# Moving Silu of z one group later and small vector work to ScalarE in a fused Mamba and mixture-of-experts kernel

## The chip, the core and the metric

The kernel runs on one core of a Trainium2 chip. The metric is device time in microseconds (us) for one launch, as a median of repeated runs. A profiled execution of the same program gives the trace; its own time stands beside its span in the table below.

## What is computed

Input `x` is 8 sequences of 1024 tokens with 256 features, float32. Two sublayers run, each with layer norm before and after:

```
x = x + layernorm(mamba(layernorm(x)))
x = x + layernorm(moe(layernorm(x)))

mamba(x): xz = rms_norm(x) @ in_proj;  xb, z = split(xz)          # 512 channels each
          xc = silu(causal_conv4(xb));  dt, B, C = xc @ x_proj
          dt = softplus(dt * w + b)
          h_t = exp(dt*A) * h_(t-1) + dt * B * xc                  # 16 states per channel
          y = (sum_s h*C + xc*D) * silu(z);  return y @ out_proj + x
moe(x):   scores = sigmoid(x @ gate.T); best 2 of 4 groups, best 4 of 16 experts
          comb = chosen scores / their sum
          return sum_e comb_e * down_e(silu(gate_e x) * (up_e x))
```

## The kernel before

**Stages and groups.** The 8192 tokens are cut into 16 chunks of 512 (two to a sequence). The program is one software pipeline written out by hand: every engine walks the same list of stages `p` (-2 to 17), each of 16 groups `g`, and at each group issues what a list of `if` lines gives it. In stage `p` the scan of chunk `p` runs. Beside it stand the norm and transposes of the input of chunk `p+2` (functions `e_...`), the projections, convolution and activations of chunk `p+1` (`f_...`), the output projection, second norm and routing of chunk `p-1` (`p_...`), one expert a group for the chunks before (`gate`, `up`, `down`, `tanh`, `expert_gate`, `expert_up`, `weigh`), and the last norm (`z_...`). Experts start in group 10 of stage 1. Scans run in stages 0 to 15.

**One group on each engine.** A group is four (channel, state) tiles of 128x512. VectorE (DVE) does `expert_gate` (L1146), scan 0 (L1051), `expert_up` (L1151), scans 1, 2 and 3, then what the group has of its own, then `inputs` of the next group (L1037), a multiply of 128x2048. ScalarE (ACT) makes the factors exp(dt*A) for the scans (`decay`, L592) into two PSUM tiles, `dA0` and `dA1`, so the factor of a scan can only be made when the scan two before it is done. In group g it issues factors 2 and 3 of g, then a first lot of other work, then factors 0 and 1 of g+1, then `tanh` of the expert (L598), then a second lot. GpSimd multiplies the states with C and weighs experts. TensorE (PE) does `add_states`, `gate`, `up`, a first lot, `down` of the expert two groups before, and a second lot. Every engine runs its own list strictly in this order.

**Even and odd stages.** In an odd stage scans start from a kept state (form `hs<-dA,carry,hs`), in an even one ScalarE keeps the last column after `tanh` (`keep_ends`, L687, tile carry).

**Places that the change touches.**
- Silu of z: `f_silu_z` (L662), in the second lot of group 12 on ScalarE. z is copied out of PSUM before by `f_z` (L654), its last quarter in the first lot of group 12. Silu and Exp lie in different activation tables, so an `ACT_TABLE_LOAD` stands on each side of it; Copy, Identity and Square need no load, Exp and Tanh share one table.
- Input transposes: `e_turn` q=0 and q=1 on TensorE (L398), both in group 13, into the one PSUM bank FP (both halves use it in turn); ScalarE copies each out by `e_xT` (L630), q=0 in the second lot of group 13, q=1 in the first lot of group 14. `f_in` for 'b0' in group 14 needs both.
- Squares: `e_squares` (sum of squared differences from the mean, for chunk p+2), in the second lot of group 3; `z_squares(p-3)` in the first lot of group 3; `p_squares` 0 and 1, in the second lot of group 3 and the first of group 4. All write their squares to the tile DX and the sums to n_sq (the line of the squares themselves is L602, or L713 for `p_squares`).
- Variances and roots: VectorE turns sums into variances (L984, L976) and runs eight small dependent steps of Newton's method (`newton`, L958 to L972): `norms` at the end of group 4, `p_scale2` at the end of group 6, `z_scale` in the last stages.
- Routing: `route_groups` and `route_experts` on VectorE at the end of group 9, 26 small instructions; the last (L1142) scales the chosen scores into `comb`. TensorE turns `comb` in group 10 (L475), ScalarE copies it out (L753).
- The gate of y: `y_out` (L1058) at the end of groups 1, 5, 9 and 13 on VectorE. `conv` (2.3 us, L1004) is at the end of groups 2 and 3, in stages -1 to 14.

Of the kernel before, what the change touches and what calls it, by code (L numbers as in the profile page):

```python
# [85 lines left out]
def sandwich_kernel(nc, x, w_in, w_out, w_gu, w_dn, w_x, w_rt, cols, alog, ebias, consts, sel_dt, out):  # L86
    with ExitStack() as ctx:
# [20 lines left out]
        def channels(t, c):  # L108
# [72 lines left out]
        n_dve = Steps(sem('n_dve'), ['var_r', 'var'] + rsqrt_names('r') + ['nb'])  # L181
        e_act = Steps(sem('e_act'), ['sum', 'nm', 'sq', 'xr'])
        f_act = Steps(sem('f_act'), ['xT0', 'xT1', 'raw0', 'tap0', 'raw1', 'tap1', 'raw2', 'tap2', 'raw3', 'tap3', 'z0', 'silu_x', 'xd', 'dt', 'z1', 'z2', 'z3', 'silu_z'],
            ['xT0', 'xT1', 'raw0', 'tap0', 'raw1', 'tap1', 'raw2', 'raw3', 'tap2', 'tap3', 'silu_x', 'z0', 'xd', 'dt', 'z1', 'z2', 'z3', 'silu_z'])
# [195 lines left out]
        def _(pe):  # L380
# [157 lines left out]
            for p, g, G in groups():  # L538
# [23 lines left out]
                if in_e(p) and g == 13:  # L562
                    e_turn(p, 0)
# [12 lines left out]
                if in_e(p) and g == 13:  # L576
                    e_turn(p, 1)
# [5 lines left out]
        def _(act):  # L583
# [20 lines left out]

            dx_half = [flat[:, (TB + b) * DM:(TB + b + 1) * DM] for b in range(TB)]
# [8 lines left out]
            def e_squares(c):  # L614
# [5 lines left out]
                squares(xin, n_sq[:, 0:TB], n_nm[:, c % 4, TB:2 * TB], dx_half).then_inc(e_act.sem, 1)  # L620

# [83 lines left out]
            def p_squares(p, k):  # L705
# [42 lines left out]

            def p_cmT(p):
# [3 lines left out]
                act.activation(cmT[:, :], FP[0:NE, :], ACT.Copy).then_inc(p_act.sem, 1)  # L753
# [10 lines left out]
            def z_squares(c):  # L764
                if c < NC - 2:
                    act.wait_ge(st_dx, 16 * min(c + 4, NC))
                    nm, sq, waste = (n_nm[:, (c + 5) % 4, 3 * TB:], n_sq[:, 2 * TB:], dx_half)
                else:
                    act.wait_ge(st_dt, 16 * NC)
                    act.wait_ge(f_dve.sem, f_dve.at(NC - 1, 'dx'))  # L770
                    nm, sq, waste = (z_s[:, 2, :], z_s[:, 1, :], xb_half)
# [3 lines left out]
                squares(my, sq, nm, waste).then_inc(z_act.sem, 1)  # L775

# [42 lines left out]
            for p, g, G in groups():  # L819
# [48 lines left out]
                if 0 <= p + 2 < NC and g == 3:  # L868
                    e_squares(p + 2)
# [68 lines left out]
        def _(dve):  # L938
# [36 lines left out]
            def variance(v, sq):  # L975
                return dve.tensor_scalar(v, sq, 1.0 / DM, LN_EPS, ALU.mult, ALU.add)  # L976

            def norms(p):
# [3 lines left out]
                if E:  # L982
                    dve.wait_ge(e_act.sem, e_act.at(i, 'sq'))
                    dve.tensor_scalar(n_v[:, 0:TB], n_sq[:, 0:TB], (1.0 + RMS_EPS) / DM, LN_EPS * RMS_EPS, ALU.mult, ALU.add).then_inc(n_dve.sem, 1)  # L984
                if Z:
                    dve.wait_ge(z_act.sem, z_act.at(p - 3, 'sq'))
                if R_:
                    dve.wait_ge(p_act.sem, p_act.at(p - 1, 'sq'))
                v0 = max(c0, TB)
                variance(n_v[:, v0:c1], n_sq[:, v0 - TB:c1 - TB]).then_inc(n_dve.sem, 1 if E else 2)  # L990
                dve.wait_ge(n_dve.sem, n_dve.at(i, 'var'))
# [23 lines left out]
            def f_dx(p):  # L1015
# [5 lines left out]
                if in_p(p):  # L1021
                    dve.wait_ge(p_dve.sem, p_dve.at(p - 1, 'comb'))
# [89 lines left out]
            def route_experts(p):  # L1112
# [136 lines left out]
```

## Time and profile before

| what | value |
|---|---|
| median of 3 runs | 2586.57 us (2585.44 to 2588.78) |
| the profiled execution: its time | 2586.42 us |
| its span in the trace | 2584.6 us |
| busy: PE, DVE, ACT, POOL | 2365.7, 2375.5, 1607.1, 1495.0 us |
| stage 7, from its `f_dx` group on (1179.9 to 1329.5) | 149.6 us |

Times in the trace are from the start of the span. "PE", "DVE", "ACT" and "POOL" are TensorE, VectorE, ScalarE and GpSimd. A timeline row gives start, duration, engine, line, operation, output and inputs, how many instructions are merged in it, and in brackets how long the engine sat idle before it and what released it. An instruction's duration reaches about 0.1 us into the next one of its engine, so costs are best taken from start to start.

### The profile page before, as it was taken

Reading aid. Unit: us, or ns where it says so; the run is one execution under the profiler, and the core shown is the slowest. Engines: PE = TensorE matmul, PEld = TensorE weight load, DVE = VectorE, ACT = ScalarE, POOL = GpSimd, SP = SyncE. Lnnn points to the kernel's source line nnn. Section 1 sums busy time; section 2 is a strip of 40 time slices with the busy share of each in tenths; the row PEclk is TensorE's granted clock in tenths of the full one; section 3 lists DMA queues with packets and bytes.
Section 4 is the critical chain, followed back from the end, with each engine's and each line's share of the span. In section 5 each row is a group of like instructions: output and inputs, shape, how many; then the busy total and the mean of one; then the engine's idle time right before and its main releaser. Section 6 shows DMA issues by size and latency. Waiting matters only on the chain.

```text
span 2584.6 us, 26581 instructions
## 1 busy us (share of the span) xinstructions
PE 2365.7 (92%) x8416; PEld 1172.9 (45%) x8416; DVE 2375.5 (92%) x2821; ACT 1607.1 (62%) x3202; POOL 1495.0 (58%) x531
## 2 busy tenths in 40 slices
PE   5556899999999999999999999999999999988988
PEld 2112354544545454454545445454545545443554
DVE  3999999999999999999999999999999999999542
ACT  6566567675766666675766667666666756654231
POOL 0554566657565665666566666656666566666421
PEclk9768899999999999999999999999999999999999
DMA  4441433535353453535354353524444452543231
GB/s 154 163 147 69 144 130 124 177 98 186 113 160 120 139 168 103 180 117 166 110 157 150 104 179 118 184 95 156 149 126 159 122 183 84 166 133 96 72 76 57
DMA packets 172759, 344.48 MB, mean 133 GB/s; under 512 B 16043, under 2 KB 81356, under 8 KB 164172
## 3 DMA queue, kind: packets, MB, share of 16 engines
q1 hardware_dynamic: 164700, 334.93, 38.5%
q0 software_dynamic: 7920, 7.87, 2.3%
q8 instruction: 67, 1.10, 0.2%
q14 instruction: 72, 0.59, 0.1%
HBM read 291.35 MB, written 51.38 MB: 133 GB/s over the span
## 4 chain that ended last, share of the span: by engine, by line
DVE 63%; issue 18%; PE 10%; ACT 8%; DMA 1%; POOL 0%; DVEq 0%; SPq 0%; ACTq 0%; POOLq 0%
DVE hs L1051 29%; DVE hs L1037 14%; DVE th L1151 5%; DVE th L1146 5%; PE MY L503 2%; PE Gp L485 2%; PE Up L493 2%; DVE XC L1004 2%; ACT dA L592 1%; ACT SZ L665 1%; DVE SZ L1058 1%; ACT L592 1%; DVE DX L1026 1%; ACT L665 1%; PE FP L410 1%
## 5 line engine op out<-in xcount | busy, mean ns | idle before, releaser
L924 POOL TENSOR_TENSOR hs<-hs,Cb 128x2048 f32<-128x2048 f32 x256 | 1159.8, 4531 | 163.6 <-DVE hs L1037 163.6
L592 ACT ACTIVATE dA<-dtr,A 128x512 f32<-128x512 f32 x1024 | 700.7, 689 | 734.5 <-DVE hs L1051 732.2
L909 POOL TENSOR_TENSOR th<-th,cmb 128x512 f32<-128x512 f32 x256 | 326.3, 1278 | 906.2 <-DVE hs L1037 804.5
L1051 DVE TENSOR_TENSOR_SCAN hs<-dA,carry,hs 128x512 f32<-128x512 f32 x512 | 627.2, 1265 | 5.9 <-ACT dA L592 5.5
L1051 DVE TENSOR_TENSOR_SCAN hs<-dA,hs 128x512 f32<-128x512 f32 x512 | 595.3, 1204 | 14.9 <-ACT dA L592 14.4
L1037 DVE TENSOR_TENSOR hs<-dxr,Bb 128x2048 f32<-128x2048 f32 x256 | 588.7, 2300 | 6.9 <-DMA dxr<-dx_d 5.1
L485 PE MATMUL Gp<-x2T,Wgu 128*128 128x512 f32 x1024 | 510.0, 621 | 27.7 <-DVE th L1146 26.8
L503 PE MATMUL MY<-Wdn,th 128*128 128x256 f32 x2048 | 485.8, 381 | 2.0 <-POOL th L909 2.0
L493 PE MATMUL Up<-x2T,Wgu 128*128 128x512 f32 x1024 | 482.7, 594 | 0.0
L503 PEld LDWEIGHTS MY<-Wdn,th 128*128 128x128 f32 x2048 | 383.3, 190 | 138.2 <-issue 92.5
L485 PEld LDWEIGHTS Gp<-x2T,Wgu 128*128 128x128 f32 x1024 | 176.6, 191 | 356.5 <-issue 275.4
L517 PE MATMUL Y<-hs,Cst 128*32 128x512 f32 x2048 | 283.8, 628 | 28.7 <-POOL hs L924 28.7
L493 PEld LDWEIGHTS Up<-x2T,Wgu 128*128 128x128 f32 x1024 | 191.6, 190 | 250.2 <-issue 223.1
L410 PE MATMUL FP<-xT,Win 128*128 128x512 f32 x476 | 236.7, 621 | 34.7 <-ACT SZ L654 15.7
L1146 DVE SCALAR_TENSOR_TENSOR th<-th,Gp 128x512 f32<-128x512 f32 x256 | 173.9, 679 | 63.5 <-ACT th L598 63.2
L598 ACT ACTIVATE th<-Gp 128x512 f32<-128x512 f32 x256 | 148.7, 581 | 96.5 <-PE Gp L485 78.2
L1151 DVE TENSOR_TENSOR th<-Up,th 128x512 f32<-128x512 f32 x256 | 170.4, 666 | 7.1 <-PE Up L493 6.5
L410 PEld LDWEIGHTS FP<-xT,Win 128*128 128x128 f32 x476 | 89.2, 195 | 157.5 <-issue 87.7
L448 PE MATMUL FP<-Wout,SZ 128*128 128x256 f32 x512 | 123.8, 385 | 8.5 <-ACT DX L702 8.5
L422 PE MATMUL FP<-XB,Kdiag 128*128 128x512 f32 x240 | 113.5, 617 | 9.6 <-ACT XB L638 9.6
L517 PEld LDWEIGHTS Y<-hs,Cst 128*32 128x32 f32 x2048 | 41.0, 109 | 172.4 <-issue 133.3
L448 PEld LDWEIGHTS FP<-Wout,SZ 128*128 128x128 f32 x512 | 98.8, 193 | 36.4 <-issue 14.2
(171 smaller groups left out, 1758.7 us busy)
## 6 DMA issues: line engine op xcount, KB each, us to landing
dxr<-dx_d SPq DMA_DIRECT2D x128, 512.0 KB, 7.2
dtr<-dt_d SPq DMA_DIRECT2D x64, 1024.0 KB, 5.5
cmb<-cm_d SPq DMA_DIRECT2D x256, 256.0 KB, 3.6
Wdn<-in_w_dn SPq DMA_DIRECT2D x256, 128.0 KB, 3.5
Bb<-bc_d SPq DMA_DIRECT2D x64, 256.0 KB, 3.0
Cb<-bc_d SPq DMA_DIRECT2D x64, 256.0 KB, 3.5
dt_d<-XB SPq DMA_DIRECT2D x15, 1024.0 KB, 4.3
dx_d<-DX SPq DMA_DIRECT2D x15, 1024.0 KB, 5.8
```

What stands on the lines that cost most here:

```text
L410: mm = pe.matmul(bank(p, f)[:, :], Win[:, q, c0:c0 + P], xT[:, q, :], start=q == 0, stop=q == KM - 1)
L485: mm = pe.matmul(Gp[:, :], Wgu[:, k, e, 0:DE], x2T[:, c % 2, k, :], start=k == 0, stop=k == KM - 1)
L493: mm = pe.matmul(Up[:, :], Wgu[:, k, e, DE:2 * DE], x2T[:, c % 2, k, :], start=k == 0, stop=k == KM - 1)
L503: mm = pe.matmul(MY[b // 2][:, (b % 2) * DM:(b % 2 + 1) * DM], th[:, q % NTH, b * P:(b + 1) * P], Wdn[:, q % NWD, :], start=e == 0 and b % ...
L517: mm = pe.matmul(Y[beta * CB:(beta + 1) * CB, :], sel_y, hs[:, G % NH, beta, :], start=False, stop=s == NSIG - 1, tile_position=(0, beta * ...
L592: act.activation(dA[h % 2][:, :], dtr[:, M % 2, beta, :], ACT.Exp, scale=A[:, k:k + 1]).then_inc(s_dA, 1)
L909: pool.tensor_tensor(th[:, q % NTH, :], th[:, q % NTH, :], cmb[:, q % 2, :], ALU.mult).then_inc(m_a, 1)
L924: pool.tensor_tensor(hs[:, G % NH, :, :], hs[:, G % NH, :, :], Cb[:, s, :].unsqueeze(1).broadcast_to([P, NBETA, CH]), ALU.mult).then_inc(s ...
L1037: dve.tensor_tensor(hs[:, G % NH, :, :], dxr[:, M % 2, :, :], Bb[:, s, :].unsqueeze(1).broadcast_to([P, NBETA, CH]), ALU.mult).then_inc(s_ ...
L1051: dve.tensor_tensor_scan(hv, dA[h % 2][:, :], hv, first, ALU.mult, ALU.add).then_inc(s_h, 1)
L1146: dve.scalar_tensor_tensor(out=th[:, q % NTH, :], in0=th[:, q % NTH, :], scalar=1.0, in1=Gp[:, :], op0=ALU.add, op1=ALU.mult).then_inc(m_v, 1)
L1151: dve.tensor_tensor(th[:, q % NTH, :], Up[:, :], th[:, q % NTH, :], ALU.mult).then_inc(m_w, 1)
```

## The change

1. `f_silu_z` moves from the second lot of group 12 to the second lot of group 13 (it has a semaphore of its own, `s_gate`).
2. `e_turn` 0 moves to the second lot of group 12 and `e_turn` 1 to the first lot of group 13; `e_xT` 0 moves to the second lot of group 12 and `e_xT` 1 to the first lot of group 13.
3. `e_squares` moves to the first lot of group 3, where `z_squares` stood; `z_squares` moves to the first lot of group 15 of the stage before.
4. ScalarE forms the variances (128x4 activations right behind the sums) in place of VectorE.
5. ScalarE scales the chosen weights (`p_comb`, four activations of 128x16) at the end of group 9, behind `f_softplus`, in place of L1142. The factor 0.5 goes into the copy of the turned tile.

```diff
@@ TensorE
             def p_comb(p):
-                pe.wait_ge(p_dve.sem, p_dve.at(c, 'comb'))
+                pe.wait_ge(p_act.sem, p_act.at(c, 'comb'))
...
                 if in_e(p) and g == 13:
-                    e_turn(p, 0)
+                    e_turn(p, 1)
...
-                if in_e(p) and g == 13:
-                    e_turn(p, 1)
+                if in_e(p) and g == 12:
+                    e_turn(p, 0)
@@ ScalarE
+            def variance(v, sq):
+                return act.activation(v, sq, ACT.Copy, scale=1.0 / DM, bias=LN_EPS)
...
             def e_squares(c):
...
+                act.wait_ge(e_act.sem, e_act.at(c, 'sq'))
+                act.activation(n_v[:, 0:TB], n_sq[:, 0:TB], ACT.Copy, scale=(1.0 + RMS_EPS) / DM, bias=LN_EPS * RMS_EPS)
+                variance(n_v[:, TB:2 * TB], n_sq[:, 0:TB]).then_inc(e_act.sem, 1)
...
+            def p_comb(p):
+                c = p - 1
+                act.wait_ge(p_dve.sem, p_dve.at(c, 'wr'))
+                if c > 0:
+                    act.wait_ge(fp_full, filled(p - 1, 'ct'))
+                for b in range(TB):
+                    ins = act.activation(comb[:, b * NE:(b + 1) * NE], picked[:, b, 0:NE], ACT.Copy, scale=R[:, 7, 2 * TB + b:2 * TB + b + 1])
+                ins.then_inc(p_act.sem, 1)
...
-                if in_e(p) and g == 14:
+                if in_e(p) and g == 13:
                     e_xT(p, 1)
-                if g == 3 and 0 <= p - 3 < NC - 2:
-                    z_squares(p - 3)
+                if 0 <= p + 2 < NC and g == 3:
+                    e_squares(p + 2)
+                if g == 15 and 0 <= p - 2 < NC - 2:
+                    z_squares(p - 2)
...
-                if 0 <= p + 2 < NC and g == 3:
-                    e_squares(p + 2)
...
+                if R_ and g == 9:
+                    p_comb(p)
...
-                if F and g == 12:
+                if in_e(p) and g == 12:
+                    e_xT(p, 0)
+                if F and g == 13:
                     f_silu_z(p)
-                if in_e(p) and g == 13:
-                    e_xT(p, 0)
@@ VectorE
-                    dve.wait_ge(e_act.sem, e_act.at(i, 'sq'))
-                    dve.tensor_scalar(n_v[:, 0:TB], n_sq[:, 0:TB], (1.0 + RMS_EPS) / DM, LN_EPS * RMS_EPS, ALU.mult, ALU.add).then_inc(n_dve.sem, 1)
+                    dve.wait_ge(e_act.sem, e_act.at(i, 'var'))
...
-                variance(n_v[:, v0:c1], n_sq[:, v0 - TB:c1 - TB]).then_inc(n_dve.sem, 1 if E else 2)
...
-                variance(p_w[:, 0, :], b_s[:, :]).then_inc(p_dve.sem, 1)
...
-                dve.scalar_tensor_tensor(out=per_b(comb[:, :]), in0=chosen, scalar=0.5, in1=wide(wr), op0=ALU.mult, op1=ALU.mult).then_inc(p_dve.sem, 1)
```

How the order moves. First ScalarE of an even stage before, from factors 0 and 1 of group 13 on: dA are the factors, th the tanh, carry the kept ends, SZ is z, xT the copied transposes.

```order
L592 ACTIVATE dA<-dtr,A 128x512 x2
L598 ACTIVATE th<-Gp 128x512
L687 ACTIVATE carry<-hs 128x4
L665 ACT_TABLE_LOAD
L665 ACTIVATE SZ<-SZ 128x2048
L592 ACT_TABLE_LOAD
L592 ACTIVATE dA<-dtr,A 128x512 x4
L598 ACTIVATE th<-Gp 128x512
L687 ACTIVATE carry<-hs 128x4
L630 ACTIVATE xT<-FP 128x512
```

The same place of the changed program:

```order
L593 ACTIVATE dA<-dtr,A 128x512 x2
L599 ACTIVATE th<-Gp 128x512
L694 ACTIVATE carry<-hs 128x4
L637 ACTIVATE xT<-FP 128x512
L593 ACTIVATE dA<-dtr,A 128x512 x2
L637 ACTIVATE xT<-FP 128x512
L593 ACTIVATE dA<-dtr,A 128x512 x2
L599 ACTIVATE th<-Gp 128x512
L694 ACTIVATE carry<-hs 128x4
L672 ACT_TABLE_LOAD
L672 ACTIVATE SZ<-SZ 128x2048
L593 ACT_TABLE_LOAD
```

Silu and its two loads now stand a group later, and the second copy of a transpose stands ahead of factors 0 and 1 of group 14, and so ahead of Silu.

TensorE before, from `down` of group 12 to the second transpose of group 13 (MY is `down`, Y `add_states`, Gp and Up the expert, FP<-Cst,xin the transposes):

```order
L503 MATMUL MY<-Wdn,th 128x256 x4
L517 MATMUL Y<-hs,Cst 32x512 x4
L485 MATMUL Gp<-x2T,Wgu 128x512 x2
L493 MATMUL Up<-x2T,Wgu 128x512 x2
L398 MATMUL FP<-Cst,xin 128x128 x4
L503 MATMUL MY<-Wdn,th 128x256 x4
L398 MATMUL FP<-Cst,xin 128x128 x4
```

and in the changed program:

```order
L504 MATMUL MY<-Wdn,th 128x256 x4
L399 MATMUL FP<-Cst,xin 128x128 x4
L518 MATMUL Y<-hs,Cst 32x512 x4
L486 MATMUL Gp<-x2T,Wgu 128x512 x2
L494 MATMUL Up<-x2T,Wgu 128x512 x2
L399 MATMUL FP<-Cst,xin 128x128 x4
L504 MATMUL MY<-Wdn,th 128x256 x4
```

The first transpose now comes ahead of the states and the expert of group 13, the second stands where the first did.

ScalarE before in group 15 (four factors with nothing between, tanh, carry, then the copies of b1; XB and XC are the convolution's input and output):

```order
L592 ACTIVATE dA<-dtr,A 128x512 x4
L598 ACTIVATE th<-Gp 128x512
L687 ACTIVATE carry<-hs 128x4
L638 ACTIVATE XB<-FP 128x512
L642 ACTIVATE XC<-FP,Cols 128x512
```

and in the changed program:

```order
L593 ACTIVATE dA<-dtr,A 128x512 x2
L793 ACTIVATE n_nm<-z_s 128x4
L603 ACTIVATE DX,n_sq<-my,n_nm 128x256 x4
L607 ACTIVATE n_v<-n_sq 128x4
L593 ACTIVATE dA<-dtr,A 128x512 x2
L599 ACTIVATE th<-Gp 128x512
L694 ACTIVATE carry<-hs 128x4
```

Six instructions of `z_squares` now stand between factor 3 of group 15 and factors 0 and 1 of the next group, ahead of its tanh.

## Rows read from the trace of the kernel before

**Rows 1.** The page, busy us of each engine (share) x instructions, whole span

```profile
PE 2365.7 (92%) x8416; PEld 1172.9 (45%) x8416; DVE 2375.5 (92%) x2821; ACT 1607.1 (62%) x3202; POOL 1495.0 (58%) x531
```

**Rows 2.** Timeline of DVE, groups 13 and 14 of odd stage 7: start, duration

```profile
1200.99 1.27 DVE L1051 TENSOR_TENSOR_SCAN hs<-dA,carry,hs 128x512 f32<-128x512 f32 x1
1203.01 2.46 DVE L1051 TENSOR_TENSOR_SCAN hs<-dA,carry,hs 128x512 f32<-128x512 f32 x2 [0.75 <-ACT dA L592]
1205.39 0.67 DVE L1058 TENSOR_TENSOR SZ<-Y,SZ 128x512 f32<-128x512 f32 x1
...
1208.17 0.68 DVE L1146 SCALAR_TENSOR_TENSOR th<-th,Gp 128x512 f32<-128x512 f32 x1
...
1210.54 3.62 DVE L1051 TENSOR_TENSOR_SCAN hs<-dA,carry,hs 128x512 f32<-128x512 f32 x3
1214.08 2.27 DVE L1037 TENSOR_TENSOR hs<-dxr,Bb 128x2048 f32<-128x2048 f32 x1
```

**Rows 3.** Timeline of ACT, end of group 12 and later, same stage

```profile
1197.18 0.58 ACT L598 ACTIVATE th<-Gp 128x512 f32<-128x512 f32 x1
1197.77 1.28 ACT L665 ACT_TABLE_LOAD   x1
1199.07 1.91 ACT L665 ACTIVATE SZ<-SZ 128x2048 f32<-128x2048 f32 x1
...
1202.29 1.30 ACT L592 ACTIVATE dA<-dtr,A 128x512 f32<-128x512 f32 x2
...
1212.48 0.58 ACT L630 ACTIVATE xT<-FP 128x512 f32<-128x512 f32 x1
```

**Rows 4.** Timeline of PE, group 13 of the same stage

```profile
1200.17 1.98 PE L485 MATMUL Gp<-x2T,Wgu 128*128 128x512 f32 x4
...
1203.71 0.60 PE L398 MATMUL FP<-Cst,xin 128*128 128x128 f32 x4
1204.15 1.89 PE L503 MATMUL MY<-Wdn,th 128*128 128x256 f32 x8
1207.25 0.66 PE L398 MATMUL FP<-Cst,xin 128*128 128x128 f32 x4 [1.21 <-ACT xT L630]
```

**Rows 5.** Timeline of ACT, DVE and PE, the same places of even stage 8

```profile
1346.14 0.58 ACT L598 ACTIVATE th<-Gp 128x512 f32<-128x512 f32 x1
...
1350.04 1.21 DVE L1051 TENSOR_TENSOR_SCAN hs<-dA,hs 128x512 f32<-128x512 f32 x1
1352.07 2.34 DVE L1051 TENSOR_TENSOR_SCAN hs<-dA,hs 128x512 f32<-128x512 f32 x2 [0.83 <-ACT dA L592]
...
1349.37 1.98 PE L485 MATMUL Gp<-x2T,Wgu 128*128 128x512 f32 x4
```

**Rows 6.** Timeline of ACT and DVE: z_squares in group 3 of stage 15

```profile
2302.29 0.20 ACT L773 ACTIVATE n_nm<-z_s 128x4 f32<-128x4 f32 x1
...
2304.51 1.28 ACT L592 ACTIVATE dA<-dtr,A 128x512 f32<-128x512 f32 x2
...
2306.34 0.69 DVE L1146 SCALAR_TENSOR_TENSOR th<-th,Gp 128x512 f32<-128x512 f32 x1 [0.90 <-ACT th L598]
```

**Rows 7.** Timeline of ACT and DVE: group 15 of stage 7, group 0 after it

```profile
1219.95 0.69 ACT L592 ACTIVATE dA<-dtr,A 128x512 f32<-128x512 f32 x1 [1.08 <-DVE hs L1051]
...
1224.37 0.68 DVE L1146 SCALAR_TENSOR_TENSOR th<-th,Gp 128x512 f32<-128x512 f32 x1
```

**Rows 8.** Timeline of ACT and DVE: norms, end of group 4 of stage 8

```profile
1267.39 0.19 ACT L713 ACTIVATION_READ_ACCUMULATOR DX<-DX,n_nm 128x1 f32 x1
...
1267.68 0.17 DVE L976 TENSOR_SCALAR n_v<-n_sq 128x12 f32<-128x12 f32 x1 [0.57 <-ACT DX L713]
1267.89 0.17 DVE L958 TENSOR_SCALAR n_rs<-n_v 128x16 int32<-128x16 int32 x1
```

**Rows 9.** Timeline of DVE: end of routing, group 9 of stage 8

```profile
1318.32 0.18 DVE L1138 RECIPROCAL DX<-DX 128x4 f32<-128x4 f32 x1
...
1318.75 0.68 DVE L1058 TENSOR_TENSOR SZ<-Y,SZ 128x512 f32<-128x512 f32 x1
```

More of the change, by code:

```diff
@@ L179, in sandwich_kernel @@
         banks = [FP, Gp, Up, MY[0], MY[1]]
[L181 to L184, printed above, removed]
+        n_dve = Steps(sem('n_dve'), rsqrt_names('r') + ['nb'])
+        e_act = Steps(sem('e_act'), ['sum', 'nm', 'sq', 'var', 'xr'])
+        f_act = Steps(sem('f_act'), ['xT0', 'xT1', 'raw0', 'tap0', 'raw1', 'tap1', 'raw2', 'tap2', 'raw3', 'tap3', 'z0', 'silu_x', 'xd', 'dt', 'z1', 'z2', 'z3'],
+            ['xT0', 'xT1', 'raw0', 'tap0', 'raw1', 'tap1', 'raw2', 'raw3', 'tap2', 'tap3', 'silu_x', 'z0', 'xd', 'dt', 'z1', 'z2', 'z3'])
+        s_gate = sem('s_gate')
         f_dve = Steps(sem('f_dve'), [f'c{k}{m}' for m in DVE_CONV for k in range(HIST)] + ['hist', 'dx'])
@@ L664, in f_silu_z @@
                 act.wait_ge(f_act.sem, f_act.at(c, 'z3'))
-                act.activation(SZ[:, c % 2, :, :], SZ[:, c % 2, :, :], ACT.Silu).then_inc(f_act.sem, 1)
+                act.activation(SZ[:, c % 2, :, :], SZ[:, c % 2, :, :], ACT.Silu).then_inc(s_gate, 1)
             def f_xd(p):
@@ L715, in p_squares @@
                     ins.then_inc(p_act.sem, 1)
+                    act.wait_ge(p_act.sem, p_act.at(c, 'sq'))
+                    variance(n_v[:, 2 * TB:3 * TB], n_sq[:, TB:2 * TB]).then_inc(p_act.sem, 1)
             def p_squares2(p):
@@ L719, in p_squares2 @@
                 squares(x1[:, (p - 1) % 2, :, :], b_s, n_nm[:, (p - 1) % 4, TB:2 * TB], dx_half).then_inc(p_act.sem, 1)
+                act.wait_ge(p_act.sem, p_act.at(p - 1, 'sq2'))
+                variance(p_w[:, 0, :], b_s[:, :]).then_inc(p_act.sem, 1)
             def p_ro(p):
@@ L752, in p_cmT @@
                     act.wait_ge(st_cm, 16 * (p - 1))
-                act.activation(cmT[:, :], FP[0:NE, :], ACT.Copy).then_inc(p_act.sem, 1)
+                act.activation(cmT[:, :], FP[0:NE, :], ACT.Copy, scale=0.5).then_inc(p_act.sem, 1)
             def z_my(c):
@@ L775, in z_squares @@
                 squares(my, sq, nm, waste).then_inc(z_act.sem, 1)
+                act.wait_ge(z_act.sem, z_act.at(c, 'sq'))
+                variance(v, sq).then_inc(z_act.sem, 1)
             def z_norm(c):
@@ L973, in newton @@
                 done('y1')
-            def variance(v, sq):
-                return dve.tensor_scalar(v, sq, 1.0 / DM, LN_EPS, ALU.mult, ALU.add)
             def norms(p):
@@ L1021, in f_dx @@
                 if in_p(p):
-                    dve.wait_ge(p_dve.sem, p_dve.at(p - 1, 'comb'))
+                    dve.wait_ge(p_act.sem, p_act.at(p - 1, 'comb'))
                 if c == 0:
@@ L1056, in y_out @@
                 if m == 0:
-                    dve.wait_ge(f_act.sem, f_act.at(c, 'silu_z'))
+                    dve.wait_ge(s_gate, c + 1)
                 dve.tensor_tensor(SZ[:, c % 2, m, :], Y[:, :], SZ[:, c % 2, m, :], ALU.mult).then_inc(y_gate, 1)
@@ L1154, in z_scale @@
                 k = c - (NC - 2)
-                dve.wait_ge(z_act.sem, z_act.at(c, 'sq'))
-                variance(z_w[:, 0, :], z_s[:, 1, :]).then_inc(z_dve.sem, 1)
-                dve.wait_ge(z_dve.sem, z_dve.at(k, 'w1'))
+                dve.wait_ge(z_act.sem, z_act.at(c, 'var'))
                 newton(z_dve, k, 'r', z_w[:, 0, :], z_w[:, 1, :], z_w[:, 2, :])
```

26 lines of the change are left out of this document (10 added, 16 removed).

## The prediction

> **What bounds the kernel now.** I read the page's busy times first, then every idle time of VectorE in its timeline, then the timelines of ScalarE and TensorE around each of those. VectorE and TensorE are both busy 92% of the span [rows 1]; nearly all of the idle time of VectorE lies before stage 0 and in the last stages. In the stages between it has just two idle times a stage. One is in group 13: scan 2 waits for its factor, 0.75 us in an odd stage and 0.83 in an even one [rows 2, 5], because Silu and its two table loads stood ahead of that factor on ScalarE [rows 3]. It is there in all 15 stages 0 to 14. The other is in `norms`, 0.57 us [rows 8], in stages 1 to 15, because the squares of the output projection end late. So a stage lasts what VectorE needs for its list plus these two waits, and the change is worth what it does to that sum. TensorE is close behind: it waits for others, but VectorE does not wait for it in stages 2 to 14.
>
> **Silu in group 13.** What a wait costs is read from start to start. Scan 1 of group 13 starts at 1200.99 and `y_out` at 1205.39, 4.40 us later; the same three scans without a wait take 3.54 (1210.54 to 1214.08) [rows 2]. The wait costs 0.86 in an odd stage; in an even one scan 1 to scan 2 is 2.03 where 1.13 is usual (1.21 less the overlap), so 0.90 [rows 5]. Moving Silu removes this. ScalarE in group 13 is then free of it: the factor for scan 2 is made once scan 0 is done, long before it is needed.
>
> The same block now stands behind tanh of group 13, and what it delays is factor 2 of group 14. From the start of tanh to the start of scan 2 the block takes 5.83 us in an odd stage (1197.18 to 1203.01) and 5.93 in an even one (1346.14 to 1352.07) [rows 2, 3, 5]. So I need when tanh starts. If nothing came between, factor 1 of group 14 would start as scan 3 ends and tanh 0.63 later. But now the copy of the second transpose stands ahead of factors 0 and 1, and it waits for TensorE. On TensorE `gate` of group 13 started at 1200.17; with the first transpose put before it (0.44, 1203.71 to 1204.15) it starts at 1200.61. From `gate` to the transpose behind `up` is 3.54 (1200.17 to 1203.71), and the transpose takes 0.60, so it ends at 1204.75 [rows 4]. ScalarE copies from 1204.79, 0.55 (0.58 less an overlap), starts two factors at 1205.34 and tanh 1.22 behind the first, at 1206.56. Scan 2 of group 14 starts 5.83 later, at 1212.39. VectorE, without the wait, starts `y_out` of group 13 at 1204.53, `expert_gate` 2.78 later at 1207.31 (tanh has ended at 1207.14, just in time), scan 1 2.37 later at 1209.68 and wants scan 2 at 1210.86 [rows 2, 3]. **The new wait is 1.5 us where 0.86 was: +0.67 in an odd stage.**
>
> In an even stage `gate` of group 13 starts at 1349.37, so with the shift the transpose ends at 1349.37 + 0.44 + 3.54 + 0.60 = 1353.95 and tanh starts at 1355.76 and ends at 1356.34 [rows 5]. VectorE's three scans take 3.54 less 3 x 0.06 there (1.21 each for 1.27), so it starts `y_out` at 1350.04 + 3.36 = 1353.40 and wants `expert_gate` 2.78 later at 1356.18: a wait of 0.19 for tanh, to 1356.37. Scan 1 follows 2.31 later and scan 2 is wanted at 1359.81; it can start at 1355.76 + 5.93 = 1361.69, so 1.88 more. Together 2.07 against 0.90: **+1.17 in an even stage.** The reason for the difference: even scans are 0.05 us shorter each, and TensorE lags more.
>
> Even stages 2 to 12 give 6 x 1.17 = 7.0, odd stages 3 to 13 give 6 x 0.67 = 4.0. In stage 1 experts have only just begun, TensorE is less behind, and I take 0. Stage 14 has no transposes; there tanh starts right after scan 3 and the wait is some 0.4 where 0.90 was, -0.5; for stage 0 I take -0.4. Sum **+10.1**. The lower end of this term is that of no lag at all: -0.6 and -0.5 a stage, -8; the upper end is another 0.5 a stage if TensorE slips further, +16.
>
> TensorE itself loses its wait of 1.21 between the transposes [rows 4], which nobody on VectorE was waiting for: no gain.
>
> **Squares of z in group 15.** Before, this block of 2.22 us (2302.29 to 2304.51) stood in group 3, where VectorE has the convolution of 2.3 us as cover. Stage 15 has no convolution, and there the block made `expert_gate` wait 0.90 [rows 6]. Group 15 has no such cover either. Factor 3 of group 15 starts at 1219.95; the block can start 0.63 later, lasts 2.22, and the variance behind it adds 0.24 (a small activation that must wait for the last sum); from the first factor to `expert_gate` is 1.83 in [rows 6]. That gives 1219.95 + 0.63 + 2.22 + 0.24 + 1.83 = 1224.87, against 1224.37 now [rows 7]. **+0.50 in each of the 13 stages 2 to 14, +6.5.** Stage 15 no longer has the block in group 3: -0.9. In group 3 the squares of the input take the freed place; they are as long, plus two small activations, and the convolution covers them; what follows them is done earlier but feeds nothing that ends last.
>
> **Variances on ScalarE.** In `norms` the last sum is read out at 1267.39 and ends at 1267.58. VectorE starts its variance at 1267.68 and Newton's first step at 1267.89 [rows 8]. ScalarE will start the variance about 0.04 behind the sum, take 0.2, and VectorE starts Newton at about 1267.85. The wait stays, the work in it changes engine: -0.04 x 15 = -0.6. The two removed instructions lay in the shadow of the wait. Their bounds are 0 and the 0.57 plus 0.21 of the rows. In `p_scale2` the sums are early, and one dependent small step of 0.2 goes (the step from 1267.68 to 1267.89 is the nearest row): -0.2 x 15 = -3.0.
>
> **Scaling the weights.** `y_out` started 0.43 behind the reciprocal [rows 9]; without L1142 between, it starts 0.10 behind it (0.18 less the overlap): -0.33 x 15 = -5.0. On ScalarE the four activations stand behind Softplus and ahead of the table load for Exp; factor 2 of group 10 is only wanted 4 us later, and TensorE turns `comb` some 7 us later, so the added 0.6 is hidden. If the cover were gone it would cost at most those 0.6.
>
> The page "Perfetto Trace Analysis" of the Trainium skill, section "Optimizing Scalar/DVE Operations", says that if VectorE is saturated, offloading work to ScalarE may make sense. By that rule all four removed instructions would count, the pair in `norms` too, for some 0.4 x 15 = 6 us more of gain than I give; the row on the wait speaks against it for that pair.
>
> **Before stage 0 and at the end.** ScalarE's two variances stand in its own chain ahead of stage 0, +0.4. At the end one collision goes and one step is added; I take 0.
>
> **Sum.** 10.1 + 6.5 - 0.9 - 0.6 - 3.0 - 5.0 + 0.4 = +7.5 us. On the profiled execution, 2586.4, that is 2593.9; the median of the runs is 0.15 above it: **2594 us**, 0.29% slower.
>
> **Rivals.** (a) The copy of the second transpose is not late, since TensorE does not lag as I think. Then the silu term is -8, and the sum -10.6 (-8 in the place of +10.1): 2576. For it: group 13 ends with `y_out`, 0.6 us in which a delayed factor costs nothing, and group 12 has no such end. Against it: TensorE stands back to back through group 13 [rows 4]. (b) All is hidden: neither copy nor squares of z delay a tanh. Then another 6.5 goes, 2569: VectorE is saturated, and each instruction that it loses is time won. The rule on offloading of the Trainium skill, page "Perfetto Trace Analysis", section "Optimizing Scalar/DVE Operations", would have it so. (c) Only the squares of z are hidden, since the factors of group 0 could be earlier than I think: +1.0, 2587. (d) TensorE slips further: the first transpose, now ahead of `gate` of group 13, meets a bank that is freed late, and every later instruction with it. It decides from 0.2 us on, as tanh has no slack in group 14. With 0.5 in 12 stages that is 2600 (7.5 + 6).
>
> **How the numbers follow.** I give my forecast 0.55, (a) 0.15, (b) 0.06, (c) 0.12, (d) 0.12. The range 2576 to 2602 leaves out (b) and half of (a), and takes in the upper end of the silu term. A measurement can tell about 0.2% from no change, 5 us; the forecast lies 2 us beyond that, and I give 0.10 of its chance to no change. So slower 0.57, same 0.22, faster 0.21. For slower alone the range is 2591 to 2602.
>
> **What would show it.** In the changed trace, VectorE should have no idle time at scan 2 of group 13, and about 1.5 us (odd) and 1.9 us (even) at scan 2 of group 14, with the second copy of a transpose on ScalarE released by TensorE. `expert_gate` of group 0 should wait 0.5 us for tanh. Newton's first step in `norms` should still wait for ScalarE. If the wait in group 14 is under 0.5, (a) was right. If there is no wait in group 0, (c). `y_out` should follow the reciprocal directly.

## The result, and the profile after

| what | before | after |
|---|---|---|
| median of 20 runs each | 2585.18 us (2581.38 to 2588.78) | 2590.11 us (2588.41 to 2591.72) |
| ratio of the two | | 1.0018 (1.0011 to 1.0025) |
| the profiled execution: its time, its span | 2586.42, 2584.6 us | 2589.84, 2588.0 us |

The medians are 4.9 us apart, and the ratio says 0.18%: slower beyond doubt, but just under the 0.2% that was set as the bound of "no change". 2594 was forecast. The measured 2590.11 lies within 2576 to 2602, but so does the time of the kernel before, and it lies 0.9 us below the 2591 to 2602 given for "slower" alone. In spans the loss is 3.4 us, with 7.5 forecast. So the total says little; what the forecast is worth must be seen term by term.

The page of the changed kernel. Columns as in [rows 1], then groups of instructions with busy time, mean ns and idle time before them:

```profile
PE 2363.5 (91%) x8416; PEld 1172.3 (45%) x8416; DVE 2360.4 (91%) x2752; ACT 1632.0 (63%) x3346; POOL 1493.6 (58%) x531
...
L1068 DVE TENSOR_TENSOR_SCAN hs<-dA,carry,hs 128x512 f32<-128x512 f32 x512 | 627.0, 1265 | 9.6 <-ACT dA L593 9.2
L1068 DVE TENSOR_TENSOR_SCAN hs<-dA,hs 128x512 f32<-128x512 f32 x512 | 595.1, 1202 | 19.2 <-ACT dA L593 18.7
...
L1157 DVE SCALAR_TENSOR_TENSOR th<-th,Gp 128x512 f32<-128x512 f32 x256 | 173.9, 679 | 71.1 <-ACT th L599 70.4
```

Against [rows 1], VectorE works 15.1 us less, and the span is longer. So the work did leave VectorE, and more than all of it came back as waiting. The same three groups of before had 5.9, 14.9 and 63.5 us of idle time:

```profile
L1051 DVE TENSOR_TENSOR_SCAN hs<-dA,carry,hs 128x512 f32<-128x512 f32 x512 | 627.2, 1265 | 5.9 <-ACT dA L592 5.5
L1051 DVE TENSOR_TENSOR_SCAN hs<-dA,hs 128x512 f32<-128x512 f32 x512 | 595.3, 1204 | 14.9 <-ACT dA L592 14.4
L1146 DVE SCALAR_TENSOR_TENSOR th<-th,Gp 128x512 f32<-128x512 f32 x256 | 173.9, 679 | 63.5 <-ACT th L598 63.2
```

**Groups 13 and 14, odd stage 7** (answers [rows 2]). The timeline of VectorE and, at 1204.29 to 1211.13, of ScalarE (answers [rows 3]):

```profile
1200.50 3.62 DVE L1068 TENSOR_TENSOR_SCAN hs<-dA,carry,hs 128x512 f32<-128x512 f32 x3
1204.04 0.67 DVE L1075 TENSOR_TENSOR SZ<-Y,SZ 128x512 f32<-128x512 f32 x1
...
1211.86 2.46 DVE L1068 TENSOR_TENSOR_SCAN hs<-dA,carry,hs 128x512 f32<-128x512 f32 x2 [1.39 <-ACT dA L593]
...
1204.29 0.60 ACT L637 ACTIVATE xT<-FP 128x512 f32<-128x512 f32 x1 [1.79 <-PE FP L399]
1204.79 1.29 ACT L593 ACTIVATE dA<-dtr,A 128x512 f32<-128x512 f32 x2
1206.01 0.58 ACT L599 ACTIVATE th<-Gp 128x512 f32<-128x512 f32 x1
...
1211.13 1.30 ACT L593 ACTIVATE dA<-dtr,A 128x512 f32<-128x512 f32 x2
```

In group 13 the three scans take 3.54 to `y_out` and wait for nothing. In group 14 scan 2 waits 1.39. The cause stands in the first ScalarE row: the second copy of a transpose waited 1.79 for TensorE, and factors 0 and 1, tanh and Silu all stand behind it.

TensorE there (answers [rows 4]): the transpose ends at 1204.26, with `gate` and `up` back to back ahead of it.

```profile
1200.12 1.98 PE L486 MATMUL Gp<-x2T,Wgu 128*128 128x512 f32 x4
1201.94 1.88 PE L494 MATMUL Up<-x2T,Wgu 128*128 128x512 f32 x4
1203.66 0.60 PE L399 MATMUL FP<-Cst,xin 128*128 128x128 f32 x4
```

**The same place of even stage 8** (answers [rows 5]):

```profile
1353.28 0.66 DVE L1075 TENSOR_TENSOR SZ<-Y,SZ 128x512 f32<-128x512 f32 x1
...
1361.55 2.34 DVE L1068 TENSOR_TENSOR_SCAN hs<-dA,hs 128x512 f32<-128x512 f32 x2 [1.80 <-ACT dA L593]
...
1355.60 0.58 ACT L599 ACTIVATE th<-Gp 128x512 f32<-128x512 f32 x1
```

**Group 15 of stage 7 and group 0 after it** (answers [rows 7]). Six instructions of `z_squares` end with the variance, two factors follow, then tanh, and `expert_gate` waits for it:

```profile
1223.06 0.21 ACT L607 ACTIVATE n_v<-n_sq 128x4 f32<-128x4 f32 x1
...
1224.39 0.57 ACT L599 ACTIVATE th<-Gp 128x512 f32<-128x512 f32 x1
...
1225.00 0.69 DVE L1157 SCALAR_TENSOR_TENSOR th<-th,Gp 128x512 f32<-128x512 f32 x1 [0.41 <-ACT th L599]
...
1230.68 2.26 DVE L1054 TENSOR_TENSOR hs<-dxr,Bb 128x2048 f32<-128x2048 f32 x1
```

**`norms` of stage 8** (answers [rows 8]): the variance is on ScalarE, and Newton's first step waits 1.04 where `norms` waited 0.57 for the sum.

```profile
1267.89 0.19 ACT L720 ACTIVATION_READ_ACCUMULATOR DX<-DX,n_nm 128x1 f32 x1
1268.11 0.20 ACT L607 ACTIVATE n_v<-n_sq 128x4 f32<-128x4 f32 x1
...
1268.44 0.17 DVE L982 TENSOR_SCALAR n_rs<-n_v 128x16 int32<-128x16 int32 x1 [1.04 <-ACT n_v L607]
```

**End of routing** (answers [rows 9]): `y_out` directly behind the reciprocal.

```profile
1318.58 0.18 DVE L1153 RECIPROCAL DX<-DX 128x4 f32<-128x4 f32 x1
1318.67 0.66 DVE L1075 TENSOR_TENSOR SZ<-Y,SZ 128x512 f32<-128x512 f32 x1
```

**A ledger.** The 256 multiplies `inputs`, one a group, serve as marks. For each I took its start after less its start before; where this difference grows between two neighbours, time was lost there, where it falls, gained. An entry of a group below is this step over that group. Over the whole program:

| place | forecast | measured |
|---|---|---|
| Silu and transposes, odd stages 3 to 13: -0.86, +1.49 each | +4.0 | +3.8 |
| the same, even stages 2 to 12: -0.94, +2.07 each | +7.0 | +6.8 |
| the same, stages 0, 1 and 14 | -0.9 | -0.9 |
| squares of z in group 15, 13 times +0.48 | +6.5 | +6.3 |
| no squares of z in stage 15 | -0.9 | -1.0 |
| variances in `norms`, mostly +0.05 each | -0.6 | +0.7 |
| variances in `p_scale2`, -0.21 each | -3.0 | -3.2 |
| scaling of the weights, -0.36 each | -5.0 | -5.6 |
| before the first `inputs` | +0.4 | +0.4 |
| 13 multiplies behind a wait, shorter | none | -1.7 |
| `y_out` of group 5, even stages 4 to 14, -0.07 to -0.12 | none | -0.5 |
| stage 2, waits for TensorE gone | none | -1.7 |
| other places of stages 0 and 1 | none | -1.2 |
| behind the last `inputs` | 0 | +1.3 |
| all other entries, each under 0.03 | none | -0.2 |
| sum (of the terms before rounding) | +7.5 | +3.4 |

### The profile page after: what moved, and what is told of

It reads as the page before. It is cut to its first block, busy times and chain, and to the rows that moved or that the text cites. A ratio compares the mean times of both kernels' runs of the same rounds, so it can differ in the third digit from the quotient of the medians.

```text
span 2588.0 us, 26658 instructions
## 1 busy us (share of the span) xinstructions
PE 2363.5 (91%) x8416; PEld 1172.3 (45%) x8416; DVE 2360.4 (91%) x2752; ACT 1632.0 (63%) x3346; POOL 1493.6 (58%) x531
## 4 chain that ended last, share of the span: by engine, by line
DVE 56%; issue 16%; PE 16%; ACT 12%; DMA 1%; POOL 0%; DVEq 0%; SPq 0%; ACTq 0%; POOLq 0%
DVE hs L1068 25%; DVE hs L1054 12%; DVE th L1162 5%; DVE th L1157 4%; PE MY L504 4%; PE Gp L486 3%; PE Up L494 3%; ACT dA L593 3%; PE FP L411 2%; DVE XC L1021 2%; ACT DX L603 1%; PE Y L518 1%; ACT SZ L672 1%; DVE SZ L1075 1%; ACT L593 1%
```

## The experiments

Every kernel below computes the whole of what the reference asks. The first four were timed on one chip against 27 runs of the kernel before (2585.87 us), the last three on another against 15 (2586.98 us). Differences to the changed kernel are taken to its 2590.11 us, and as the kernel before had 2585.18 in the series above, they are good to 1 or 2 us.

**1. Silu and transposes as before.** In the changed program, `f_silu_z`, `e_turn` and `e_xT` go back to their old groups:

```diff
-                if in_e(p) and g == 12:
-                    e_xT(p, 0)
-                if F and g == 13:
+                if F and g == 12:
                     f_silu_z(p)
+                if in_e(p) and g == 13:
+                    e_xT(p, 0)
```

(and `e_xT` 1 in group 14, `e_turn` 0 and 1 in group 13).

> The changed kernel with Silu of z and both input transposes and their copies where they were before; the squares, variances and the scaling of the weights stay as changed. Theory (the late copy delays Silu): the wait at scan 2 of group 14 (1.39 us odd, 1.80 even) goes and the one of group 13 (0.75, 0.83) is back; per stage -0.63 odd and -1.13 even against the changed kernel, in all 2590.1 - 10.5, about 2580, ratio to the kernel before 0.998. Rival (the waits are not what sets the stage, so the squares alone made it slower): under 2 us off the changed kernel, 2588 or more.

Measured: 2583.83 us, ratio 0.9995 (0.9987 to 1.0004). It is 6.3 us under the changed kernel, so the move is a loss, by less than the 10 expected. In the trace the two entries of groups 13 and 14 are 0.00 in every steady stage, as expected. So the 9.8 us of these entries did come back, but three things stand against them. Seven multiplies that followed the wait of group 14 in even stages are long again (+0.9; see the unexpected findings), the stretch before the first `inputs`, which differs from one execution to the next, is 2.0 longer, and in stage 2 two waits for TensorE are back (+1.6). So the spans are only 4.7 apart. The kernel before has the first of them too:

```profile
337.99 0.69 DVE L1058 TENSOR_TENSOR SZ<-Y,SZ 128x512 f32<-128x512 f32 x1 [0.96 <-PE Y L517]
```

and in this experiment:

```profile
338.72 0.69 DVE L1075 TENSOR_TENSOR SZ<-Y,SZ 128x512 f32<-128x512 f32 x1 [0.96 <-PE Y L518]
```

With the transposes where the change puts them, the same `y_out` starts with no wait:

```profile
335.36 0.66 DVE L1075 TENSOR_TENSOR SZ<-Y,SZ 128x512 f32<-128x512 f32 x1
```

That is worth 1.07 and 0.55 us in groups 1 and 5 of stage 2, once in the program. So the moved transposes also gave something: work taken earlier on TensorE, at the one place where VectorE waited for TensorE.

**2. Only the second copy of a transpose back.** One line, and the transposes themselves and Silu stay where the change puts them:

```diff
-                if in_e(p) and g == 13:
+                if in_e(p) and g == 14:
                     e_xT(p, 1)
```

> The changed kernel with one thing undone: the copy of the second transpose (e_xT 1) stands in the first lot of group 14 again, behind Silu. Theory (late copy): the tanh of group 13 starts right after scan 3, the wait at scan 2 of group 14 falls from 1.39 to about 0.2 us odd and from 1.80 plus a late expert_gate to about 0.4 even; -1.25 and -1.65 us a stage, 2590.1 - 17 = about 2573. Rival (Silu and its two table loads are what is too long, whatever stands ahead of them): the wait stays at 0.8 or more in group 14, about 2580. TensorE will wait about 1 us for the copy in group 14 before b0, at no cost.

Measured: 2573.54 us, ratio 0.9953 (0.994 to 0.9965), 16.6 us under the changed kernel. One instruction of 0.6 us, put behind the factors in place of ahead of them, decides the sign of the whole change. The timeline of even stage 8:

```profile
1345.23 0.58 ACT L599 ACTIVATE th<-Gp 128x512 f32<-128x512 f32 x1
...
1350.44 1.30 ACT L593 ACTIVATE dA<-dtr,A 128x512 f32<-128x512 f32 x2
1351.68 0.58 ACT L637 ACTIVATE xT<-FP 128x512 f32<-128x512 f32 x1
...
1351.16 2.34 DVE L1068 TENSOR_TENSOR_SCAN hs<-dA,hs 128x512 f32<-128x512 f32 x2 [0.37 <-ACT dA L593]
```

Tanh starts 0.63 behind the last factor, the copy stands behind factor 3 of group 14 and waits for nothing, and scan 2 waits 0.37 instead of 1.80 (0.16 instead of 1.39 in odd stage 7). Against the kernel before, the ledger has +0.26 (odd) and +0.47 (even) in group 14 and -0.86 and -0.93 in group 13: with the copy out of its way, the move of Silu is a gain of 0.60 and 0.46 a stage.

**3. The squares as before.** `z_squares` back to the first lot of group 3, `e_squares` to the second:

```diff
-                if 0 <= p + 2 < NC and g == 3:
-                    e_squares(p + 2)
-                if g == 15 and 0 <= p - 2 < NC - 2:
-                    z_squares(p - 2)
+                if g == 3 and 0 <= p - 3 < NC - 2:
+                    z_squares(p - 3)
...
+                if 0 <= p + 2 < NC and g == 3:
+                    e_squares(p + 2)
```

> The changed kernel with the squares of z and of the input back in group 3, in the lots they had before. Theory (the squares of z have no cover in group 15): the wait of 0.40 us of expert_gate in group 0 goes; VectorE gains 0.35 to 0.48 us in 13 stages, loses 0.9 in group 3 of stage 15; 2590.1 - 4.5 = about 2585.6. Rival (the wait in group 0 only takes up slack that another wait would take, as GpSimd is still busy then): under 1 us less than the changed kernel.

Measured: 2586.60 us, ratio 1.0003 (0.9994 to 1.0011), 3.5 us under the changed kernel, where 4.5 were expected; the spans are 4.5 apart. The ledger has 0.00 in group 0 where it had +0.48, and the squares of z in group 3 of stage 15 cost 1.2 again. But in even stages the multiply after it is long again:

```profile
1227.78 2.39 DVE L1054 TENSOR_TENSOR hs<-dxr,Bb 128x2048 f32<-128x2048 f32 x1
```

It was 2.26 in the changed kernel (the row at 1230.68 above). So the wait of 0.48 cost 0.35 net there. What this is, is told under the unexpected findings.

**4. The last routing scaled on VectorE.** For the last chunk alone L1142 comes back (with 1.0 for 0.5, as the 0.5 stays in the copy of the turned tile), TensorE waits for VectorE there, and ScalarE does no `p_comb` in stage 16:

```diff
-                if R_ and g == 9:
+                if R_ and g == 9 and p < NC:
                     p_comb(p)
...
+                if c == NC - 1:
...
+                    dve.scalar_tensor_tensor(out=per_b(comb[:, :]), in0=chosen, scalar=1.0, in1=wide(wr), op0=ALU.mult, op1=ALU.mult).then_inc(p_dve.sem, 1)
```

> The changed kernel, but in the last routing (stage 16) VectorE scales the chosen weights, as before. Theory (there ScalarE waits for VectorE with tanh of an expert queued behind, and TensorE for both): the 1.3 us that the end lost come back, 2588.8; the last 90 us of the trace stand as those of the kernel before. Rival (the loss at the end is the later store of the turned weights, which the added activation work delays by 0.5): 0.5 us or less.

Measured: 2589.15 us, ratio 1.0013 (1.0004 to 1.0022). The 1.0 us is less than runs scatter, so the trace decides. In the changed kernel, ScalarE, VectorE and TensorE in stage 16:

```profile
2490.92 0.90 ACT L766 ACTIVATE comb<-picked,DX 128x16 f32<-128x16 f32 x4 [5.56 <-DVE DX L1153]
2491.73 0.57 ACT L599 ACTIVATE th<-Gp 128x512 f32<-128x512 f32 x1
...
2492.34 0.69 DVE L1157 SCALAR_TENSOR_TENSOR th<-th,Gp 128x512 f32<-128x512 f32 x1 [1.45 <-ACT th L599]
...
2491.97 0.60 PE L476 MATMUL FP<-Cst,comb 128*16 128x128 f32 x4 [1.90 <-ACT comb L766]
2493.08 3.12 PE L486 MATMUL Gp<-x2T,Wgu 128*128 128x512 f32 x4 [0.51 <-DVE th L1157]
```

`p_comb` is ahead of tanh in ScalarE's list and waits 5.56 for the routing, which has no scans beside it here and nothing to cover it. Tanh, ready for 3 us, waits with it. In the experiment tanh starts at 2488.52, `expert_gate` follows the routing, and `gate` starts at 2492.01:

```profile
2488.52 0.60 ACT L602 ACTIVATE th<-Gp 128x512 f32<-128x512 f32 x1 [3.03 <-PE Gp L489]
...
2491.27 0.68 DVE L1164 SCALAR_TENSOR_TENSOR th<-th,Gp 128x512 f32<-128x512 f32 x1
...
2492.01 1.98 PE L489 MATMUL Gp<-x2T,Wgu 128*128 128x512 f32 x4
```

Its span is 2.2 above that of before, and its last `inputs` is 2.2 later than before: so of the 1.3 us behind the last `inputs` nothing is left. The edit shows that `p_comb` in stage 16 is the cause. It does not separate the theory from its rival, since it frees tanh and also has the weights turned 0.6 sooner; the last section follows both paths.

**5. No new waits.** Experiments 2, 3 and 4 together: what stays of the change is Silu's and the transposes' new places, the variances and the scaling.

> The three repairs together: copy of the second transpose behind Silu (as in copy_back), squares as before (as in squares_back), last scaling on VectorE (as in tail_dve). Theory (the costs are separate and add up): 2573.5 - 4.3 - 1.0 = about 2568, ratio 0.9935, with no wait of expert_gate in groups 14 and 0. Rival (TensorE, busy 97% of a stage, becomes the bound as VectorE's list shortens): 2572 or more, with waits of expert_gate for a tanh that waits for gate.

Measured: 2568.03 us, ratio 0.993 (0.9918 to 0.9942). That is 5.5 under experiment 2, where experiments 3 and 4 gave 3.5 and 1.0 (5.5 in spans, against 4.5 and 1.2). So the costs add up as single terms do, and no other engine takes over as the bound: the forecast of 2568 holds.

**6. The statistics of the output projection earlier.** On top of 5, `p_rev` of the second half goes between factors 2 and 3 of group 4, so that the squares behind it, and with them the variance, end sooner:

```diff
                     decay(G * NBETA + 2)
+                    if R_ and g == 4:
+                        p_rev(p, 1)
                     decay(G * NBETA + 3)
...
-                if R_ and g in (3, 4):
+                if R_ and (g == 3 or g == 4 and p == NC):
                     p_rev(p, g - 3)
```

> no_waits with one more move: the copy of the second half of the output projection (p_rev 1, 0.8 us) stands between factors 2 and 3 of group 4 instead of behind both. Theory (norms waits for ScalarE's last squares and the variance behind them, so only what ends these sooner is a gain): they end 0.6 to 0.8 us sooner, factor 3 comes 0.2 late but scan 3 does not wait; the wait in norms of about 1 us falls to 0.3; -0.65 in 15 stages, about 10 us less than no_waits, 2558. Rival (the gap is kept by TensorE, whose second half of the output projection is late): under 2 us less.

Measured: 2563.48 us, ratio 0.9911 (0.9897 to 0.9924): 4.5 under experiment 5, where 10 were expected, and the fastest of all. Newton's wait falls in both kinds of stage (odd 0.93 to 0.36, even 0.95 to 0.43), but only the odd ones gain that much. An even stage of experiment 5 and of this one, from scan 1 on:

```profile
1252.47 3.54 DVE L1071 TENSOR_TENSOR_SCAN hs<-dA,hs 128x512 f32<-128x512 f32 x3
1256.96 0.17 DVE L985 TENSOR_SCALAR n_rs<-n_v 128x16 int32<-128x16 int32 x1 [0.95 <-ACT n_v L610]
```

```profile
1252.70 3.78 DVE L1073 TENSOR_TENSOR_SCAN hs<-dA,hs 128x512 f32<-128x512 f32 x3
1256.90 0.17 DVE L987 TENSOR_SCALAR n_rs<-n_v 128x16 int32<-128x16 int32 x1 [0.43 <-ACT n_v L610]
```

The three scans take 0.24 longer: factor 3, now behind `p_rev`, ends at 1255.22 where scan 3 could have begun at about 1254.96. So the expectation that scan 3 would not wait fails in even stages. The ledger, against experiment 5, has -0.57 in odd stages and -0.3 in most even ones, some 6 us in all; the profiled execution gives back 2.7 of that before stage 1, the medians differ by 4.5.

**7. The variances alone.** The kernel before with part 4 of the change only (the factor 0.5 also stays in the copy of the turned tile, which adds and removes no instruction):

```diff
+            def variance(v, sq):
+                return act.activation(v, sq, ACT.Copy, scale=1.0 / DM, bias=LN_EPS)
...
-                variance(n_v[:, v0:c1], n_sq[:, v0 - TB:c1 - TB]).then_inc(n_dve.sem, 1 if E else 2)
...
-                variance(p_w[:, 0, :], b_s[:, :]).then_inc(p_dve.sem, 1)
```

> The kernel before with part 4 of the change alone: variances on ScalarE. Theory (in norms the removed vector work lay in the shadow of the wait, in p_scale2 it did not): +0.05 us a stage at the end of group 4, -0.2 at the end of group 6; -2.3 in all, ratio 0.999. Rival (VectorE is saturated, so both count): -0.4 to -0.6 a stage, 6 to 9 us less.

Measured: 2584.58 us, ratio 0.9992 (0.9983 to 1.0001), which by itself can't be told from no change. The ledger can: about +0.06 in `norms` (+0.19 and +0.24 in the last two stages), -0.20 in `p_scale2` in every stage. In even stages `y_out` of group 5 gives back 0.07, as in the changed kernel. Newton's first step in stage 8:

```profile
1266.87 0.17 DVE L980 TENSOR_SCALAR n_rs<-n_v 128x16 int32<-128x16 int32 x1 [0.96 <-ACT n_v L607]
```

So two instructions taken off VectorE in `norms` are worth nothing, and one in `p_scale2` is worth its whole 0.2, on an engine that is busy 92% of the span.

## Why the prediction was right, point by point

**The bound.** VectorE's list plus its waits: right. Every term that moved a wait or an instruction there shows in the ledger, and experiment 5 took 22 us from the changed kernel with no other engine stepping in. But "VectorE does not wait for it in stages 2 to 14", said of TensorE, was a misreading: the trace of before has `y_out` waiting 0.96 and 0.55 us for TensorE in stage 2 (at 337.99 and 378.04).

**Silu in group 13.** Right to 0.1 us at each step of the chain. Stage 7 ran 0.5 us ahead of the working's times by then; with that taken off, the transpose was to end at 1204.25 and ended at 1204.26, tanh to start at 1206.06 and started at 1206.01, scan 2 to start at 1211.89 and started at 1211.86. In stage 8 (0.1 ahead) tanh was to start at 1355.64 and did at 1355.60, scan 2 at 1361.57 and did at 1361.55. The term was +10.1 and is +9.8. Experiment 2 shows the mechanism: take the copy out of the way and 16.6 us come back; the working's "no lag at all", rival (a), had said 18 (from 2594 to 2576).

**Squares of z.** +0.50 forecast, +0.48 measured in each stage. By then this stage ran 0.15 behind the working's times (factor 3 at 1220.10 for 1219.95); with that added, `expert_gate` was to start at 1225.02 and started at 1225.00. What was left out is the shorter multiply behind the wait, which gives back 0.13 in even stages.

**Variances.** The forecast that the wait in `norms` stays and swallows both removed instructions was right, where the Trainium skill ("Perfetto Trace Analysis", "Optimizing Scalar/DVE Operations") says, with no further condition, that offloading to ScalarE may make sense when VectorE is saturated: experiment 7 shows +0.06 for two of them and -0.20 for the third. The sign was wrong by 0.1 us: the variance was to start 0.04 behind the sum, which it did (1268.11 behind 1268.08), but VectorE started 0.13 behind its end (1268.31 to 1268.44) where 0.03 had been assumed, though the row of before had shown 0.10 for such a hand-over (1267.58 to 1267.68).

**Scaling of the weights.** -0.36 for -0.33: right.

**The step that failed: "At the end one collision goes and one step is added; I take 0."** It is +1.3 us, shown by experiment 4. The working had looked at who waits for `comb` and found TensorE 7 us later, and factor 2 of group 10 4 us later. Both hold in stages with scans. In stage 16 there are none, and the instruction queued behind the waiting `p_comb` is tanh, whose input was ready 3 us before; `comb` itself is turned 0.6 later too. The working named the cover, but didn't ask where the cover is missing. How 1.2 us at `gate` become 1.3 at the end is in the last section.

**Not in the working at all,** -5.2 us together, and more than the distance of forecast to result: the waits for TensorE in stage 2 (-1.7; experiment 1 brings back 1.6), the shorter multiplies (-1.7), the small step of `y_out` in group 5 (-0.5), and -1.2 in stages 0 and 1. The last I can't assign: waits for loads there differ from execution to execution, and the start of the first `inputs` lies between -0.7 and +2.4 us of that of before in the eight traces.

**How good the number is.** The terms that the working priced at other than 0 sum to +7.5 and measured +7.5. That the sums agree so closely is luck: `norms` cost 1.3 more than forecast, and all the others together 1.3 less. What the working left out or took as 0 gave back 4.1, more than half, so the loss came out at 3.4 in spans. The sign is owed to the mechanism, above all to the two large terms; that the time still fell into the range is owed in part to the width of the range.

## What to carry to other kernels

An instruction that waits in an engine's strict order is priced by what is queued behind it, not by its own length: the copy of 0.6 us that waited 1.8 for TensorE cost 16.6 us a launch, and its release was one line. Before work leaves a busy engine, look whether it stands in the shadow of a wait; there it is worth nothing, elsewhere its whole start-to-start step. And ask of each cover in which stages it is missing, at the ends of a pipeline above all.

## What the runs showed of the hardware that was not expected

**A multiply on VectorE is longer while GpSimd still multiplies.** Before, between groups 0 and 1 of stage 8, GpSimd and VectorE:

```profile
1225.76 4.52 POOL L924 TENSOR_TENSOR hs<-hs,Cb 128x2048 f32<-128x2048 f32 x1
...
1230.04 2.39 DVE L1037 TENSOR_TENSOR hs<-dxr,Bb 128x2048 f32<-128x2048 f32 x1
```

GpSimd ends at 1230.28, 0.24 into VectorE's multiply, which takes 2.39. After, `expert_gate` has waited, GpSimd (1225.90 and 4.52) ends at 1230.42 before the multiply begins at 1230.68, and it takes 2.26. The same holds at the end of group 14 of stage 6 (2.40 at 1063.02 before, 2.27 at 1062.70 after, behind the new wait). It holds for all of them: in the kernel before, 49 of the 256 multiplies begin while GpSimd's has more than 0.15 us to go, and they take 2.38 to 2.41; the other 207 take 2.26 to 2.29. In the changed kernel these are 36 (2.37 to 2.41) and 220 (2.26 to 2.29), so 13 fewer are long, 1.7 us in all. So a small wait of VectorE that ends such an overlap costs 0.13 less than its length. The Trainium skill, "Perfetto Trace Analysis", "Optimizing Scalar/DVE Operations", says that GpSimd and VectorE share a read port of the on-chip memory, which agrees. Scans that ran wholly beside GpSimd's multiply kept their 1.2 us. No run changed the overlap alone, so the cause is argued, not shown; the next finding shows the same pair of engines with a larger effect.

**A small step of VectorE that meets a multiply of GpSimd lasts until that ends.** At the end of the program VectorE does Newton's steps for the last norm, 128x4 each and 0.16 to 0.17 us long, while GpSimd does its first multiply with the new weights. From experiment 4 and from experiment 3:

```profile
2498.99 1.11 DVE L987 SCALAR_TENSOR_TENSOR z_w<-z_w 128x4 f32<-128x4 f32 x1
```

```profile
2495.72 1.25 POOL L933 TENSOR_TENSOR th<-th,cmb 128x512 f32<-128x512 f32 x1 [18.94 <-DMA cmb<-cm_d]
...
2495.83 1.17 DVE L986 TENSOR_TENSOR z_w<-z_w 128x4 f32<-128x4 f32 x1
```

In experiment 4 GpSimd's multiply runs from 2498.81 to 2500.07, and the step ends at 2500.10. In six of the nine traces a step begins while 0.8 us or more of this multiply are to go; it takes 0.9 to 1.3 us and ends 0.02 to 0.03 behind the multiply. In the other three, the changed kernel among them, the steps begin within 0.04 of its end, and all are short. So it holds as often as the two met, but here too no run changed the overlap alone.

**How the wait in stage 16 reaches the end, and TensorE's clock.** In the changed kernel TensorE was busy 0.67 us of the 3 from 2490 to 2493, and the `gate` after it took 3.12 for four matmuls. In experiment 3, which has the same `p_comb` in stage 16, it was busy 0.69 of 3 at the same place, and `gate` took 1.98. The granted clock (us, PE, PEld, DVE, ACT and POOL busy, clock, DMA share, GB/s), first the changed kernel, then experiment 3:

```profile
2490.00:2493.00 3.00, 0.67 (x5) 0.30 (x4) 1.45 (x5) 1.78 (x6) 0.00 (x0) 1.00 0.00 0
2493.00:2496.30 3.30, 3.22 (x5) 1.45 (x6) 0.71 (x2) 0.25 (x2) 0.00 (x0) 0.62 0.06 15
```

```profile
2485.55:2488.55 3.00, 0.69 (x5) 0.29 (x4) 1.45 (x5) 1.75 (x6) 0.00 (x0) 1.00 0.00 0
2488.55:2491.85 3.30, 3.19 (x8) 1.44 (x8) 1.29 (x3) 1.39 (x6) 0.00 (x0) 1.00 0.06 15
```

After nearly the same idle stretch the clock is 0.62 as a mean in one (so mostly at the lower of its two levels, 1.2 of 2.4 GHz) and stays whole in the other. What decides this, the runs don't show. But they show what the slower clock cost. Times from the start of the last `inputs`:

| what | experiment 4 | changed kernel | experiment 3 |
|---|---|---|---|
| `gate` starts, takes | 73.19, 1.98 | 74.38, 3.12 | 74.41, 1.98 |
| the next tanh | 75.21 | 77.54 | 76.43 |
| Newton's first step | 79.96 | 82.29 | 81.18 |
| GpSimd's multiply ends | 81.25 | 82.28 | 82.73 |
| Newton's longest step | 1.11 | 0.17 | 1.17 |
| the step behind Newton | 82.49 | 83.87 | 83.77 |
| end of the program | 167.96 | 169.33 | 169.25 |

With the slower clock the loss is 1.4 us, without it 1.3, though the clock makes tanh 1.1 later. Two paths meet in Newton's steps. One goes from `gate` over tanh and the squares of z on ScalarE. The other is the expected rival's: the turned weights are stored and loaded again, and GpSimd multiplies with them, which holds the Newton step that it meets. From there both go on to the last norm on ScalarE, to GpSimd, which sends the result out before it multiplies again, and to `down` on TensorE. In experiments 3 and 4 the second path comes last and costs a step 1.0 us. In the changed kernel tanh is so late that Newton's steps miss the multiply, which gives back most of what the clock took. The load of experiment 3 landed 0.4 later than that of the changed kernel. So, as an estimate from these three traces, 0.9 to 1.3 us of the loss belong to the wait behind `p_comb` and 0.1 to 0.5 to the clock.
